# Four biased squares on ScalarE instead of batch-norm statistics on VectorE, in the key pass of a four-stage transformer kernel

## The reference, cut to what matters

```
def _layernorm(x, axis=-1, eps=1e-05):
    m = jnp.mean(x, axis=axis, keepdims=True)
    v = jnp.var(x, axis=axis, keepdims=True)
    return (x - m) / jnp.sqrt(v + eps)

x = x + _layernorm(_L0_attn_ref(_layernorm(x), ...))
x = x + _layernorm(_L0_ffn_ref(_layernorm(x), ...))
x = x + _layernorm(_L1_attn_ref(_layernorm(x), ...))
x = x + _layernorm(_L1_ffn_ref(_layernorm(x), ...))
```

## Time and profile before

| | |
|---|---|
| time, median of 3 runs | 680.41 us (678.76 to 682.44) |
| profiled execution | 683.49 us, span 681.7 us |
| busy share of the span | PE 76%, DVE 59%, ACT 52%, POOL 46% |
| key pass in the trace | about 243.7 us (first squares) to 318.5 us |
| mean granted TensorE clock | 0.865 of full speed |

### The profile page before, as it was taken

The page is one execution under the profiler, slowest core; times in us unless marked ns, Lnnn a source line. Parts: engine busy times, 40 slices in busy tenths (PEclk is TensorE's granted clock), DMA queues, the critical chain, the costliest instruction groups (busy, mean ns, idle before and its releaser), DMA issues.

```text
span 681.7 us, 13654 instructions
## 1 busy us (share of the span) xinstructions
PE 519.0 (76%) x3941; PEld 382.7 (56%) x3943; DVE 400.6 (59%) x1565; ACT 354.5 (52%) x848; POOL 310.6 (46%) x332
## 2 busy tenths in 40 slices
PE   1748646388786518888999993369999999999925
PEld 1446315356564414443343442269999999999922
DVE  4789758845332339996247878944455555544434
ACT  3823634344343236664366752546666666666623
POOL 3604300157888735541011211047677766667534
PEclk9976765589898859999799996579999999999967
DMA  8501259112333321100001011111111111111156
GB/s 198 136 0 34 66 196 391 13 42 45 48 41 44 32 66 33 32 1 1 1 1 31 17 32 31 17 29 48 47 48 49 47 47 47 49 44 51 37 188 197
DMA packets 47288, 42.24 MB, mean 62 GB/s; under 512 B 15345, under 2 KB 41322, under 8 KB 46730
## 3 DMA queue, kind: packets, MB, share of 16 engines
q1 hardware_dynamic: 31658, 25.35, 11.6%
q0 software_dynamic: 10368, 15.82, 10.4%
q10 hardware_dynamic: 5216, 0.52, 0.5%
HBM read 26.23 MB, written 15.30 MB: 61 GB/s over the span
## 4 chain that ended last, share of the span: by engine, by line
PE 47%; DVE 21%; ACT 9%; issue 8%; POOL 7%; DMA 5%; ACTq 1%; SPq 0%; DVEq 0%; POOLq 0%
PE bank L1973 19%; PE banks L1994 5%; PE bank L1994 5%; POOL sum_dram L692 4%; ACT arena L979 2%; PE bank L1887 2%; PE bank L1781 2%; POOL arena L676 2%; ACT xnf L802 2%; DVE st L1060 1%; PE bank L1920 1%; DVE arena L1384 1%; ACT row L921 1%; DVE hit L1196 1%; DMA wgu<-y_dram 1%
## 5 line engine op out<-in xcount | busy, mean ns | idle before, releaser
L1973 PE MATMUL bank<-arena 128*128 128x128 f32 x1136 | 140.4, 278 | 0.4 <-ACT arena L1034 0.4
L1973 PEld LDWEIGHTS bank<-arena 128*128 128x128 f32 x1136 | 134.2, 194 | 0.7 <-ACT arena L1034 0.7
L1590 DVE TENSOR_TENSOR arena<-arena,bank 128x512 f32<-128x512 f32 x71 | 48.8, 688 | 82.1 <-PE bank L1973 82.1
L771 POOL DMA_INDIRECT y_dram<-arena,sidx x71 | 69.9, 985 | 44.3 <-DVE arena L1595 40.7
L1020 ACT ACTIVATE arena<-wgu 128x1024 f32 x71 | 74.9, 1057 | 26.6 <-PE bank L1973 26.2
L763 POOL DMA_INDIRECT arena<-x3row_dram,gidx x71 | 68.8, 969 | 40.9 <-issue 21.0
L709 POOL TENSOR_TENSOR rstd<-ve,mhalf 128x4 f32<-128x4 f32 x23 | 24.1, 1049 | 91.7 <-DVE ve L1341 89.8
L1026 ACT ACTIVATE arena<-bank 128x512 f32<-128x512 f32 x71 | 42.4, 597 | 42.7 <-PE bank L1973 42.7
L676 POOL DMA_INDIRECT arena<-x1row_dram,idx x32 | 31.4, 982 | 43.8 <-DVE idx L1293 34.3
L692 POOL DMA_INDIRECT sum_dram<-arena,idx x28 | 44.2, 1577 | 10.8 <-issue 8.2
L979 ACT ACTIVATE arena<-bank 128x512 f32<-128x512 f32 x64 | 33.0, 602 | 23.8 <-PE bank L1887 23.8
(11 more groups left out here) (384 smaller groups left out, 1141.8 us busy)
## 6 DMA issues: line engine op xcount, KB each, us to landing
wgu<-in_wgu SPq DMA_DIRECT2D x1, 4096.0 KB, 23.5
wgu<-y_dram SPq DMA_DIRECT2D x8, 512.0 KB, 6.9
X<-in_x SPq DMA_DIRECT2D x8, 256.0 KB, 5.1
sum_dram<-zero POOLq DMA_DIRECT2D x8, 256.0 KB, 4.2
x1row_dram<-row SPq DMA_DIRECT2D x8, 256.0 KB, 2.4
w<-in_w SPq DMA_DIRECT2D x1, 2048.0 KB, 9.4
arena<-in_wd SPq DMA_DIRECT2D x1, 2048.0 KB, 14.2
acc<-sum_dram SPq DMA_DIRECT2D x8, 256.0 KB, 2.9
```

The source lines that it names most:

```text
L771: nc.gpsimd.indirect_dma_start(y_dram, bass.IndirectOffsetOnAxis(ap=sidx1[:, o.n:o.n + 1].bitcast(U32), axis=0), yr[:, o.ring], None).then ...
L1590: nc.vector.tensor_tensor(gl[:, m.pair], sgl[:, m.pair], bank[3 + m.pair][:], ALU.mult).then_inc(f_gated, 1)
L1973: last = nc.tensor.matmul(bank[first + m.pair][:, h * P:(h + 1) * P], wnow[:, m.pair, at_:at_ + P], xrT[:, m.ring], start=True, stop=True)
```

## The change

VectorE no longer computes mean and variance of x2 by batch-norm statistics. ScalarE squares x2 with a bias per token instead: with scale D^-0.5 and the bias -mu * D^-0.5, the sum over a row of Square(scale * x + bias) is the variance. The four squares (one per tile) of group m+2 stand between `evict(1)` and `evict(2)`, and write their sums into the variance places of `mv` (named `xv`). VectorE gets one small instruction that makes the bias (`mub`) from `mu` in front of the x2 update, takes the mean for `nmr` from `mu` instead of `mv`, and its two small instructions on the variance (add epsilon, then the maximum) now stand between the key products of tiles 2 and 3. The semaphore `d_fvar` now counts both kinds of squares, so the counts waited for are worked out by `of_sums` and `of_x2`.

```
+        xv = mv[:, :, :, 1]
+        mub = eq[:, 0:2 * J].rearrange("p (u j) -> p u j", u=2)
+        def of_sums(h):
+            return 1 if early(h, 1) else 2 * h.n
+        def of_x2(g):
+            return 2 * g.n + 3
 # GpSimd
-                    power_of_squares(frstd[:, h.b], h.b, d_fvar, h.n + 1, d_frstd)
+                    power_of_squares(frstd[:, h.b], h.b, d_fvar, of_sums(h), d_frstd)
 # ScalarE
                     squares_of(lambda j: acc[:, h.b, j], row, h.b, d_fvar)
+                if u:
+                    act.wait_ge(d_x2, LEAD + u.n + 1)
+                    if not early(u, 2):
+                        act.wait_ge(d_xvar, LEAD + u.n - 1)
                 evict(1)
+                if u:
+                    squares_of(lambda j: X[...][:, ds(J * u.place + j, 1)]...,
+                               row, u.b, d_fvar, mub[:, u.b], xv, 1 if h else 2)
                 evict(2)
 # VectorE
                     dve.wait_ge(d_frstd, LEAD + g.n + 1)
+                    nc.vector.tensor_scalar(mub[:, g.b], mu[:, ds(g.place, 1)]..., -float(D) ** -0.5, None, ALU.mult)
                     ...
                 if f:
-                    shift(f.b, d_xrstd, f.n + 1, d_xnmr)
+                    dve.wait_ge(d_xrstd, LEAD + f.n + 1)
+                    nc.vector.scalar_tensor_tensor(nmr[:, f.b], mu[:, ds(f.place, 1)]..., -1.0,
+                                                   rstd[:, f.b], ALU.mult, ALU.mult).then_inc(d_xnmr, 1)
                 key_products(m, 0)
+                key_products(m, 1)
+                key_products(m, 2)
                 if g:
-                    dve.wait_ge(d_x2, LEAD + g.n + 1)
+                    dve.wait_ge(d_fvar, LEAD + of_x2(g))
                     if not early(g, 2):
                         dve.wait_ge(d_std, LEAD + g.n - 1)
-                    stats1(lambda j: xl[:, ds(g.place, 1), j]..., g.b, None)
-
-                    nc.vector.scalar_tensor_tensor(ve[:, g.b], ve[:, g.b], 1e-24 / D, mv[:, g.b, :, 1], ALU.mult,
+                    do(nc.vector.tensor_scalar(ve[:, g.b], xv[:, g.b], EPS, None, ALU.add))
+                    nc.vector.scalar_tensor_tensor(ve[:, g.b], ve[:, g.b], 1e-24 / D, xv[:, g.b], ALU.mult,
                                                    ALU.max).then_inc(d_xvar, 1)
-                key_products(m, 1)
-                key_products(m, 2)
                 key_products(m, 3)
```

More of the change, by code:

```diff
@@ L168, in program @@
         hit = sb("hit", [P, SEG])
[L169 to L174, removed]
         mvx = hit[:, 0:64].rearrange("p (c b j s) -> p c b j s", c=CH, b=NB, j=J)
@@ L179, in program @@
         eq = sb("eq", [P, SEG])
+        mu = sb("mu", [P, GR, J])
+        mu_at = mu[:].rearrange("p (b c) j -> p c b j", b=NB)
+        fv = sb("fv", [P, 2, J])
+        xv = mv[:, :, :, 1]
+        mub = eq[:, 0:2 * J].rearrange("p (u j) -> p u j", u=2)
+        frstd = sb("frstd", [P, 2, J])
+        eps = sb("eps", [P, J])
+        wsum = sb("wsum", [P, NB])
         rank = sb("rank", [P, SEG])
@@ L917, in tokens, with squares_of @@
                     "p o d -> p (o d)")
-            def squares_of(src, out, u, done, bias=None):
+            def squares_of(src, out, u, done, bias=None, sums=fv, by=1):
                 for j in range(J):
                     last = nc.scalar.activation(out[:, u, j], src(j), ACT.Square, scale=float(D) ** -0.5,
-                                                bias=0.0 if bias is None else bias[:, j:j + 1], accum_out=fv[:, u, j:j + 1])
-                last.then_inc(done, 1)
+                                                bias=0.0 if bias is None else bias[:, j:j + 1], accum_out=sums[:, u, j:j + 1])
+                last.then_inc(done, by)
             def key_pass(at):
-                h, g, m = at(3), at(1), at(0)
+                h, u, g, m = at(3), at(2), at(1), at(0)
                 def evict(j):
@@ L950, in key_pass @@
                     squares_of(lambda j: acc[:, h.b, j], row, h.b, d_fvar)
+                if u:
+                    act.wait_ge(d_x2, LEAD + u.n + 1)
+                    if not early(u, 2):
+                        act.wait_ge(d_xvar, LEAD + u.n - 1)
                 evict(1)
+                if u:
+                    squares_of(lambda j: X[:].rearrange("p b c (j d) -> p (b c j) d", j=J)[:, ds(J * u.place + j, 1)].rearrange(
+                        "p o d -> p (o d)"), row, u.b, d_fvar, mub[:, u.b], xv,
+                               1 if h else 2)
                 evict(2)
@@ L1389, in key_pass @@
                     dve.wait_ge(d_frstd, LEAD + g.n + 1)
+                    nc.vector.tensor_scalar(mub[:, g.b], mu[:, ds(g.place, 1)].rearrange("p o j -> p (o j)"), -float(D) ** -0.5,
+                                            None, ALU.mult)
                     for j in range(J):
@@ L1394, in key_pass @@
                 if f:
-                    shift(f.b, d_xrstd, f.n + 1, d_xnmr)
+                    dve.wait_ge(d_xrstd, LEAD + f.n + 1)
+                    nc.vector.scalar_tensor_tensor(nmr[:, f.b], mu[:, ds(f.place, 1)].rearrange("p o j -> p (o j)"), -1.0,
+                                                   rstd[:, f.b], ALU.mult, ALU.mult).then_inc(d_xnmr, 1)
                 key_products(m, 0)
+                key_products(m, 1)
+                key_products(m, 2)
                 if g:
-                    dve.wait_ge(d_x2, LEAD + g.n + 1)
+                    dve.wait_ge(d_fvar, LEAD + of_x2(g))
                     if not early(g, 2):
                         dve.wait_ge(d_std, LEAD + g.n - 1)
-                    stats1(lambda j: xl[:, ds(g.place, 1), j].rearrange("p o d -> p (o d)"), g.b, None)
-                    nc.vector.scalar_tensor_tensor(ve[:, g.b], ve[:, g.b], 1e-24 / D, mv[:, g.b, :, 1], ALU.mult,
+                    do(nc.vector.tensor_scalar(ve[:, g.b], xv[:, g.b], EPS, None, ALU.add))
+                    nc.vector.scalar_tensor_tensor(ve[:, g.b], ve[:, g.b], 1e-24 / D, xv[:, g.b], ALU.mult,
                                                    ALU.max).then_inc(d_xvar, 1)
-                key_products(m, 1)
-                key_products(m, 2)
                 key_products(m, 3)
-            groups(dve, key_pass, 2, 0, 2, ch, 3)
+            groups(dve, key_pass, 2, 0, 2, ch, 1)
             dve.wait_ge(d_added, LEAD + J * GR)
```

## The result

| | before | after |
|---|---|---|
| time, median | 680.74 us (678.76 to 682.44, 4 runs) | 687.68 us (686.59 to 689.47, 4 runs) |
| profiled execution, its span | 683.49 us, 681.7 us | 687.63 us, 685.8 us |
| key pass, first squares to TensorE's first matmul of the next pass | 74.78 us | 82.42 us |
| from there to the first transposes of `acc` (line 1905, 1924 after) | 26.30 us | 22.41 us |

The ratio is 1.0092, with a 95% interval of 1.0071 to 1.0112. The change makes the kernel some 6.9 us slower (4.8 to 7.6 by that interval). The forecast was 8.4 us and 688.8 us.

A forecast was written before the change was run, and what follows sets the result against it. The bound was taken to be a VectorE-ScalarE loop from `nmr` to `nmr`, not VectorE's busy time. Five steps of 1.16 (5.8) with 0.5, 1.55 and 0.6 made 8.4 us, 680.41 to 688.8 us; range 683.1 to 692.9.

The forecast's parts named there:

- What bounds the pass: Steady key pass: a loop through VectorE and ScalarE, from `nmr` to the next `nmr`, sets the 8.37 us period.
- Squares, 0.64 per step: ScalarE before eviction 2: four biased squares take 1.55 us, use up 0.9 us slack and add 0.64 per step.
- Pair 0.42, bias 0.10: VectorE, in the loop: two variance instructions between key products 2 and 3 add 0.42 us, bias before x2 update 0.1.
- Five steps, 5.8 us: Steps 0 to 4, from `nmr` of group 1 to that of group 6: five times 1.16 us longer, 5.8.
- Filling, 2.05 us to the first copy: Steps -2 and -1, while the pipe fills: 0.5 us later for group 0, 1.55 for group 1's squares.
- Emptying, 0.6 us: End of the key pass, `nmr` of group 6 to normalisation of group 7: 7.63 us becomes 8.2, 0.6 later.
- Sum, 8.4 us: Whole kernel: 5.8 us with 0.5, 1.55 and 0.6 makes 8.4 us slower, median 688.8 us.
- Power at 1.97 us, hidden: GpSimd's `rstd` power behind key products 3: takes 1.97 us, fits by 0.35, costs nothing in steady steps.
- VectorE as the bound: Rival for the key pass: VectorE sets the pace and the change frees it, 9.7 us faster, 670.7 us; chance 0.04.
- Cover for the new work: Rival: squares cost 1.17 us, small instructions hide almost wholly in free time; 2 us slower, 682.4 us; chance 0.09.
- a power holds up VectorE: Rival: GpSimd's power blocks the x2 update, `nmr` 0.9 us later in six steps, 694.2 us; chance 0.04.
- The clock: Rival: longer gaps drop TensorE's granted clock from 2.4 to 1.2 GHz, two such steps give 698 us; chance 0.03.

The follow-up runs named there:

- the experiment without bias: Changed kernel with ScalarE's four squares of x2 without the bias per token, bias instruction kept on VectorE; time 1.0069 of before (1.0042 to 1.0096).
- the changed kernel's second set: The changed kernel, unchanged, run and profiled once more; time 1.0107 of the kernel before (1.0086 to 1.0128).
- the removal alone: Kernel before with only VectorE's statistics of x2 left out of the key pass, variance and mean constant; time 0.999 of before (0.9969 to 1.0011).

## Why the prediction was right

Step by step, measured in the profile of after.

- **What bounds the pass.** Right. The loop's parts sum to the period in both kernels, and taking 1.3 us off VectorE alone left it at 8.37.
- **Squares, 0.64 per step.** Measured 0.67 alone. The spacing was 0.38 to 0.39, the row of the same form at 427 us. From the kind of square already in this pass it would have been 0.4 us too cheap, and the experiment without bias shows that: 0.37 per period.
- **Pair 0.42, bias 0.10.** Measured 0.39 and 0.07 in steps of the hardware loop. In steps 0 and 1, which are written out, the pair took 0.27.
- **Five steps, 5.8 us.** Measured 5.21, from the first copy of transposed rows to `nmr` of group 6 (44.17 before, 49.38 after). The steps from group 2's `nmr` on grew by 0.99, 1.12, 1.19 and 1.12, as forecast on the whole; the 0.99 is step 1 with its cheaper pair. Step 0, counted from the first copy, grew by only 0.79 where 1.16 was costed. There the way from eviction 1 to key products 2 grew by 0.66, the pair cost 0.28 and the bias 0.05, and 0.20 came back in front of eviction 1. Nearly all of this last part is that the normalisation starts 0.39 behind eviction 0 instead of 0.55: in the kernel before it had to wait for `nmr` there, which now comes in time. This is the term that was furthest off, 0.6 of 0.8 us.
- **Filling, 2.05 us to the first copy.** Measured 1.91: the first copy comes 11.70 us behind the first squares, in the two rows below, and came 9.79 behind them (253.49 and 243.70).

```profile
244.36 0.31 ACT L929 ACTIVATE row<-acc 128x128 f32<-128x128 f32 x1 [10.09 <-DMA acc<-sum_dram]
...
256.06 0.57 ACT L973 ACTIVATE xnf<-bank 128x512 f32<-128x512 f32 x1
```

- **Emptying, 0.6 us.** Measured 0.52, from `nmr` of group 6 to the end of the pass.
- **Sum, 8.4 us.** The three measured terms make 1.91 + 5.21 + 0.52 = 7.64, all of the pass's growth. In the median of the time it was 6.9, and 7.3 in the changed kernel's second set; 7.64 lies at the upper edge of the first interval and inside the second. The high end of the range took 0.48 us for a square that doesn't overlap, which is the unbiased one; it made no difference.
- **Power at 1.97 us, hidden.** Right: it took 1.99, and `nmr` never waited for it in the loop. It waits for the last power of the pass, 0.77 us, on the path that the forecast costed for emptying. GpSimd's row in after (idle before in brackets):

```profile
284.07 1.99 POOL L717 TENSOR_TENSOR rstd<-ve,mhalf 128x4 f32<-128x4 f32 x1 [0.50 <-DVE ve L1424]
```

- **The rivals.** VectorE as the bound fell with the removal alone (its price was 9.6 us, not the 9.7 that stand there: eight times 1.2). Cover for the new work fell with key products 2, which wait 0.56. That a power holds up VectorE fell with the rows above: the power runs from 284.07 to 286.06, and the x2 update begun inside it at 285.32 took 1.13 as before. The rule weighed there (the Trainium skill, "SBUF — State Buffer", section SBUF: two separate sides) holds here for GpSimd, whose power takes 1.99 us behind a key product instead of 1.00, and not for VectorE behind a power. The clock was 0.50 of full speed while the pipe filled, up to 258 us in before and 260 in after, and 1.00 from 262 us to the end of the pass in both; in the 2 us before it rose TensorE worked 1.9 and 2.0 us. So the longer gaps of the steady steps cost no clock, and from the first copy to eviction 0, at the low clock, both kernels took the same time (2.15 and 2.13 us).

One forecast figure was off in its size only: the wait before key products 1 was to be over 2 us and is 1.97.

## What to carry to other kernels

An engine that is busy 94% of a period isn't the bound if it stands still once per period for another. Follow one value round the loop until the parts sum to the period, and cost a change by where its instructions stand in that loop. Work moved off such an engine turns into waiting there, while what is put in front of something that the loop passes through is paid for, less the slack that stood there: the squares took 1.55 us of ScalarE and added 0.67 to the period, the pair and the bias stood where there was no slack and added all of their 0.47. To gain, first take out of the loop what nobody in it waits for: moving the squares of the sums shortened the period by 0.4 us, where moving the statistics lengthened it by 1.1. The time itself isn't shown shorter by it (0.9985, up to 1.0005).

## What the runs showed of the hardware that was not expected

- Two dependent 128x4 instructions between two streams of key products cost 0.27 us in the steps written out and 0.39 in the hardware loop. The instructions are the same, and the second starts 0.19 behind the first in both. The difference lies behind the second: the key products start 0.08 after it in step 0, in the rows below, and 0.20 after it in the loop (283.77 and 283.97 above). What in the loop's code costs the rest was not tried.

```profile
264.88 0.16 DVE L1423 TENSOR_SCALAR ve<-mv 128x4 f32<-128x4 f32 x1
265.07 0.17 DVE L1424 SCALAR_TENSOR_TENSOR ve<-ve,mv 128x4 f32<-128x4 f32 x1
265.15 1.22 DVE L1400 TENSOR_TENSOR arena<-arena 128x1024 f32<-128x1024 f32 x1
```

- The stretch behind the pass took 22.4 to 26.3 us over thirteen profiled executions, and its length goes with the mean granted clock of the 26 us behind the pass: 22.4 us at 1.00 (one profile), 23.9 to 24.1 at 0.93 (four), 25.1 to 25.2 at 0.87 (six), 26.3 at 0.80 (two). The changed kernel alone gave 22.4 and 26.3. What decides the clock there stays open. The 3.9 us between them are more than half of the whole difference measured here, and a comparison of two profiled spans (4.1 us) would have hidden nearly half of what the pass lost.
